# Key norms as quadrant products of one column, and the modifiers of keys and queries in one product

## The reference, cut to what matters

```python
def _modifier(x, w1, b1, w2, b2):
    h = jax.nn.gelu(x @ w1.T + b1, approximate=False)     # w1: 48 x 192, one for each of k, q, v   <-- touched
    return h @ w2.T + b2
xn = _ln(x, ln_in_g, ln_in_b)
k = xn @ Wk.T + 0.1 * _modifier(xn, km_w1, km_b1, km_w2, km_b2)      # 12 heads x 64; q and v alike
k = _ln(k.reshape(b, s, H, HD), lnk_g, lnk_b)
def step(M, kvq):
    k_t, v_t, q_t = kvq
    out_t = einsum('bhdk,bhk->bhd', M, q_t)
    kn = k_t / (norm(k_t, axis=-1) + 1e-06)               # one norm for each token and head        <-- touched
    pred = einsum('bhdk,bhk->bhd', M, kn)
    M_new = M - einsum('bhd,bhk->bhdk', pred + lr * (pred - v_t), kn)
    return M_new, out_t
```

## Time and profile before

| | |
|---|---|
| median of 3 runs | 1339.08 us (1338.1 to 1340.39) |
| profiled execution, its own time | 1343.92 us |
| its span | 1342.0 us |
| mean granted TensorE clock | 0.963 of full speed |
| busy over the span | PE 1232.0 us (92%), PEld 986.8 (74%), DVE 815.9 (61%), ACT 726.8 (54%), POOL 518.8 (39%) |
| chain that ended last, by engine | PE 34%, POOL 31%, issue 25%, DVE 5%, the rest 5% |
| products of `key_norms` | 384 instructions of 128x2, 45.8 us busy |
| products of `modifier` (L599) | 384 instructions of 128 columns, 28.0 + 27.9 us busy |

### The profile page before, as it was taken

One profiled execution on the slowest core, in us unless ns is written; L12 is line 12 of the kernel. 1 busy time (PEld: TensorE's weight loads), 2 busy tenths in 40 slices (PEclk: granted clock), 3 DMA queues, 4 the chain that ended last, 5 costly groups with the idle time before them and its releaser, 6 DMA issues.

```text
span 1342.0 us, 45313 instructions
## 1 busy us (share of the span) xinstructions
PE 1232.0 (92%) x17572; PEld 986.8 (74%) x17572; DVE 815.9 (61%) x2120; ACT 726.8 (54%) x1955; POOL 518.8 (39%) x689
## 2 busy tenths in 40 slices
PE   5898999999998588999999999999999999999975
PEld 5765666666665377888888888888888888888864
DVE  0136433333333266887877778787777878777752
ACT  0012222222222367777777777777777777777742
POOL 0000000000000355656565565556556555655521
PEclk8998999999998589999999999999999999999986
DMA  9888999999992012212221221122122112212210
GB/s 324 304 319 295 370 381 372 375 374 373 374 375 95 15 20 39 47 32 40 48 38 35 40 50 33 37 51 38 36 41 49 32 38 50 38 35 40 42 33 15
DMA packets 219995, 179.24 MB, mean 134 GB/s; under 512 B 164342, under 2 KB 189881, under 8 KB 219321
## 3 DMA queue, kind: packets, MB, share of 16 engines
q1 hardware_dynamic: 219818, 176.79, 41.3%
HBM read 154.72 MB, written 22.02 MB: 132 GB/s over the span
## 4 chain that ended last, share of the span: by engine, by line
PE 34%; POOL 31%; issue 25%; DVE 5%; SPq 2%; DMA 1%; ACT 1%; POOLq 0%; DVEq 0%; ACTq 0%
PE PS L438 29%; POOL region L1128 14%; POOL region L1111 5%; POOL region L1116 3%; POOL region L1122 1%; PE PS L514 1%; POOL region L1078 1%; POOL region L1094 1%; POOL region L1106 1%; SPq L308 1%; POOL region L1101 1%; PE PS L692 1%; PE PS L532 1%; PE PS L599 1%; POOL region L1091 1%
## 5 line engine op out<-in xcount | busy, mean ns | idle before, releaser
L438 PE MATMUL PS<-region 64*64 64x64 f32 (+6 forms) x5864 | 354.3, 287 | 20.7 <-DVE region L1176 13.6
L438 PEld LDWEIGHTS PS<-region 64*64 64x64 f32 (+3 forms) x5864 | 230.7, 139 | 119.6 <-issue 109.8
L1128 POOL TENSOR_TENSOR region<-region,powers 128x12 f32<-128x12 f32 x96 | 223.8, 2332 | 7.5
L1057 POOL TENSOR_TENSOR region<-region,powers 128x1 f32<-128x1 f32 x32 | 6.1, 192 | 408.5 <-DVE region L1236 408.5
L692 PEld LDWEIGHTS PS<-region 64*64 64x64 f32 x4608 | 145.1, 137 | 23.0 <-issue 18.9
L692 PE MATMUL PS<-region 64*64 64x64 f32 x4608 | 157.8, 223 | 1.4 <-ACT region L938 1.4
L438 PE MATMUL PS<-cw_hi,xr_hi 128*128 128x512 f32 (+3 forms) x384 | 149.3, 389 | 6.5 <-DVE region L1379 3.1
L905 ACT ACTIVATE region<-PS 128x512 f32<-128x512 f32 (+1 forms) x192 | 93.6, 488 | 84.3 <-PE PS L438 83.7
L438 PE MATMUL PS<-cw_lo,xr_hi 128*128 128x512 f32 (+3 forms) x384 | 130.8, 341 | 0.0
L438 PE MATMUL PS<-cw_hi,xr_lo 128*128 128x512 f32 (+3 forms) x384 | 130.5, 340 | 0.0
L832 ACT ACTIVATE region<-PS 128x384 f32<-128x384 f32 x32 | 15.7, 491 | 193.2 <-PE PS L438 193.2
(11 more groups left out here) (171 smaller groups left out, 2262.8 us busy)
## 6 DMA issues: line engine op xcount, KB each, us to landing
region<-in_Wq SPq DMA_DIRECT2D x32, 1152.0 KB, 5.8
region<-in_Wk SPq DMA_DIRECT2D x32, 1152.0 KB, 8.1
region<-in_Wv SPq DMA_DIRECT2D x32, 1152.0 KB, 7.7
region<-in_x SPq DMA_DIRECT2D x32, 384.0 KB, 6.7
n_scratch<-region SPq DMA_DIRECT2D x64, 192.0 KB, 3.4
region<-h_scratch SPq DMA_DIRECT2D x64, 96.0 KB, 2.0
region<-in_w SPq DMA_DIRECT2D x2, 2304.0 KB, 13.6
region<-i_scratch SPq DMA_DIRECT2D x256, 12.0 KB, 1.8
```

The lines of the kernel that those rows point to most:

```text
L438: return nc.tensor.matmul(dst, lhsT, rhs, start=first, stop=last)
L1128: pool.tensor_tensor(rs[:, cols], rs_var[:, cols], root[:, cols], ALU.pow).then_inc(S["rs_ready"], 1)
```

## The change

`key_norms` works on quadrants. For each of the 6 head pairs it makes 4 products: for each half of the tokens (64) and each of the two heads (64 partitions) the squared keys, 64x64, are the weights and one column of ones, 64x1, is the moving operand. Even heads go to bank 6 and odd heads to bank 7, columns 500 to 505 (`NORM_AT`). That is 24 products in place of 6. Since bank 7 is in turn used by `ffn_second(m)`, `key_norms` now waits for `f2_ready` (the copy of that result, `ffn_out(m)` on VectorE), and it has a `settled` ahead of it. `weigh_out`, which writes bank 7 too, now waits for `norm_copied` of the same step. `take_norm` is two copies of 6 columns, and what waited for one count of `norm_copied` waits for two.

`modifier` makes one product for keys and queries together: the weights have 112 columns (48 of the keys, 16 of zeros, 48 of the queries), and a second product of 48 columns is for the values. That is 4 products in place of 6. The GELU of the keys reads partitions 0 to 47 and writes partitions 64 to 111, as those of queries and values do. The host lays out weights and biases to suit.

One copy of 12 columns became two of 6. The diff, cut to its core:

```diff
@@ -49,6 +49,8 @@
 BLK_PITCH = BLK * SEQ + BLK
 HEAD_PITCH = NBLK * BLK_PITCH
 EPS = 1e-5
+NORM_AT = 500
+MOD_PAIR = R2 + MOD
 
 PIECE_BANK = (0, 1, 0, 7, 7, 7)
 PIECES = [(0, 512, 0), (512, 256, 0), (768, 256, 1), (1024, 512, 1), (1536, 512, 2), (2048, 256, 2)]
@@ -143,8 +145,8 @@
         p1w = sb("p1w", [P, CH, ATT])
         weff1 = sb("weff1", [HALF, ATT])
         weff2 = sb("weff2", [HALF + 1, ATT])
-        mod1a = sb("mod1a", [P, 3 * MOD])
-        mod1b = sb("mod1b", [R2, 3 * MOD])
+        mod1a = sb("mod1a", [P, MOD_PAIR + MOD])
+        mod1b = sb("mod1b", [R2, MOD_PAIR + MOD])
         gate_a = sb("gate_a", [P, ATT])
         gate_b = sb("gate_b", [R2 + 1, ATT])
         wo = sb("wo", [P, HEADS // 2, ATT])
@@ -584,7 +586,7 @@
 
             def turn_x(x, j):
                 pe.wait_ge(S["xh_ready"], x + 1)
-                need(pe, "norm_copied", upto(j))
+                need(pe, "norm_copied", upto(j, 2))
                 need(pe, "mod_ready", 3 * x)
                 for k, src in enumerate((xh, xn)):
                     nc.tensor.transpose(PS[:, 6, 2 * k * P:2 * k * P + P], src[:, 0:P], ident)
@@ -595,9 +597,9 @@
                 pe.wait_ge(S["xlin_copied"], 2 * x + 2)
                 pe.wait_ge(S["xgate_copied"], 2 * x + 2)
                 for part, (w, rows) in enumerate(((mod1a, P), (mod1b, R2))):
-                    for m in range(3):
-                        last = nc.tensor.matmul(PS[R2:R2 + MOD, 6, m * P:(m + 1) * P], w[:, m * MOD:(m + 1) * MOD],
-                                                x_aug[0:rows, part, :], start=part == 0 and m == 0, stop=part == 1,
+                    for i, (first, cols) in enumerate(((0, slice(0, MOD_PAIR)), (R2, slice(MOD_PAIR, MOD_PAIR + MOD)))):
+                        last = nc.tensor.matmul(PS[first:MOD_PAIR, 6, i * P:(i + 1) * P], w[:, cols],
+                                                x_aug[0:rows, part, :], start=part == 0 and i == 0, stop=part == 1,
                                                 skip_group_check=True)
                 last.then_inc(S["mod_mm"], 1)
 
@@ -652,8 +654,14 @@
             def key_norms(j):
                 pe.wait_ge(S["ksq_ready"], j + 1)
                 need(pe, "mod_ready", upto(j + 1, 3))
+                need(pe, "f2_ready", upto(j - 3))
+                settled(pe)
                 for i in range(HH):
-                    last = mm(PS[:, 6, 2 * i:2 * i + 2], ksq[:, i, :], head_ones)
+                    for e in range(2):
+                        tokens = slice(64 * e, 64 * e + 64)
+                        for odd, bank in enumerate((6, 7)):
+                            rows = slice(64 * odd, 64 * odd + 64)
+                            last = mm(PS[tokens, bank, NORM_AT + i:NORM_AT + i + 1], ksq[rows, i, tokens], head_ones[rows, odd:odd + 1])
                 last.then_inc(S["norm_mm"], 1)
 
             def grams(j, half):
@@ -746,6 +754,7 @@
                 pe.wait_ge(S["outT_ready"], 2 * l + 2)
                 need(pe, "raw_ready", upto(l + 2, 6))
                 need(pe, "f2_ready", l)
+                need(pe, "norm_copied", upto(l + 2, 2))
                 for i in range(HH):
                     last = mm(PS[:, 7, 0:ATT], outT[:, i, :], wo[:, i, :], i == 0, i == HH - 1)
                 last.then_inc(S["wo_mm"], 1)
@@ -922,9 +931,9 @@
             def gelu(x):
                 act.wait_ge(S["mod_mm"], x + 1)
                 rows = slice(R2, R2 + MOD)
-                for m in range(3):
-                    act.activation(x_aug[rows, 1 + m, :], PS[rows, 6, m * P:(m + 1) * P], ACT.Gelu,
-                                   bias=mod_bias[rows, m:m + 1]).then_inc(S["mod_ready"], 1)
+                for m, (at, i) in enumerate(((slice(0, MOD), 0), (rows, 0), (rows, 1))):
+                    act.activation(x_aug[rows, 1 + m, :], PS[at, 6, i * P:(i + 1) * P], ACT.Gelu,
+                                   bias=mod_bias[at, i:i + 1]).then_inc(S["mod_ready"], 1)
 
             def odd_heads(buf, i):
                 return buf.rearrange("p (g o d) -> p g o d", o=2, d=HD)[:, :, i, :]
@@ -1106,7 +1115,7 @@
                 pool.tensor_tensor(h2b[:, :], h2[:, :], beta[:, :], ALU.add).then_inc(S["h2b_ready"], 1)
 
             def key_lengths(j):
-                pool.wait_ge(S["norm_copied"], j + 1)
+                pool.wait_ge(S["norm_copied"], 2 * j + 2)
                 need(pool, "n2", j)
                 pool.tensor_tensor(norm[:, 1, :], norm[:, 0, :], square_root[:, 0:HEADS], ALU.pow).then_inc(S["n1"], 1)
 
@@ -1420,7 +1429,8 @@
             def take_norm(j):
                 dve.wait_ge(S["norm_mm"], j + 1)
                 need(dve, "n1", j)
-                dve.tensor_copy(norm[:, 0, :], PS[:, 6, 0:HEADS]).then_inc(S["norm_copied"], 1)
+                for odd, bank in enumerate((6, 7)):
+                    dve.tensor_copy(norm[:, 0, odd:HEADS:2], PS[:, bank, NORM_AT:NORM_AT + HH]).then_inc(S["norm_copied"], 1)
 
             def inverse_norms(j):
 
@@ -1558,8 +1568,11 @@
                           twice(a["attn_lnk_g"]), twice(a["attn_lnk_b"]), twice(a["attn_lnq_g"]), twice(a["attn_lnq_b"]),
                           a["ffn_b1"]], axis=1)
     d["vecs2"] = np.stack([a["attn_ln_in_g"][P:], a["attn_ln_in_b"][P:]], axis=1)
-    d["mod_bias"] = np.stack([a[f"attn_{m}m_b1"] for m in "kqv"], axis=1)
-    d["mod1T"] = np.concatenate([a[f"attn_{m}m_w1"].T for m in "kqv"], axis=1)
+    gap = np.zeros(R2 - MOD, np.float32)
+    pairs = [np.concatenate([a["attn_km_b1"], gap, a["attn_qm_b1"]]), np.concatenate([np.zeros(R2, np.float32), a["attn_vm_b1"]])]
+    d["mod_bias"] = np.stack(pairs, axis=1)
+    k1, q1, v1 = [a[f"attn_{m}m_w1"].T for m in "kqv"]
+    d["mod1T"] = np.concatenate([k1, np.zeros((ATT, R2 - MOD), np.float32), q1, v1], axis=1)
     d["modT"] = np.concatenate([np.concatenate([a[f"attn_{m}m_w2"].T, row(a[f"attn_{m}m_b2"])]) for m in "kqv"], axis=1)
     d["kqvT"] = np.concatenate([a["attn_Wk"].T, a["attn_Wq"].T, a["attn_Wv"].T], axis=1)
     d["gateT"] = np.concatenate([a["attn_Wg"].T, row(a["attn_bg"])])
```

4 lines of the change are left out of this document (2 added, 2 removed).

## The result

The changed kernel takes 1344.33 us (median of 14 runs, 1339.90 to 1348.92), the kernel before beside it 1340.65 (14 runs, 1338.10 to 1343.87): ratio 1.0029, 95% interval 1.0016 to 1.0041. It is 3.7 us slower, more than the 0.2% that I called no change. The profiled execution has a span of 1344.0 us, 2.0 above that of before; its own time is 1345.96.

What follows compares the result with a forecast made beforehand. The prediction took a closed loop of VectorE and GpSimd as the bound, with steps unchanged at 26.15 us. Start -1.55 and end +0.2 summed to -1.35 us, giving 1337.7 us, range 1334 to 1347.

Steps and rivals of the forecast that it cites:

- The steady step, and what bounds it: Middle of the second stage: a closed loop of VectorE and GpSimd sets the step, which stays at 26.15 us.
- The norms' products: Key norms on TensorE: the block takes 0.86 us, like `read_out`, in place of 1.35, saving 0.49 us.
- The first rival: Key norms: quadrants overlap only in pairs, block 1.5 us, time 1347; decides from a block of 1.14 us on; chance 0.10.
- The new wait in the middle: Middle steps: `key_norms` wait for `ffn_out` and start 0.84 us later, grams 0.35 us late; the step pays nothing.
- The cover: Middle steps: slack absorbing the late grams, 1.9 us at `take_a` and 0.28 us left at `take_e`.
- The modifiers: Middle steps on TensorE: a third of 12 instructions goes, gain 0.35 us of 1.64, at most 0.55, at worst nothing.
- The forecast's own price for a gain of nothing: Modifiers: if mode changes drain TensorE, they gain nothing and the sum is about 0.7 us more.
- The copies: VectorE: two copies of 0.17 us in place of one, covered by 1.5 us; nothing taken, upper side +3 in all.
- The start, "together -1.55 us": Start, chain through TensorE: modifiers of tile 0 save 0.7, of tile 1 0.35, norms 0.5; between -2.0 and 0.
- The third rival: TensorE idles more before the norms and its clock falls to 1.2 GHz in places: 1.5 us a step, +40; chance 0.04.
- The end, "+0.2": Steps without `moments_h`: norm copies at 1232.6 in place of 1232.12, partly covered by VectorE's next wait; between 0 and +0.5.

Runs made afterwards that it cites:

- before_moments: The kernel before with `moments_h` on VectorE moved from behind `ffn_out` to ahead of `invert_small` of the step before: 1339.54 us, ratio 1.0009.
- before_swap: The kernel before with `moments_h` ahead of `ffn_out` on VectorE in place of behind it: 1332.97 us, ratio 0.9940.
- before_wait: The kernel before with the new wait of `key_norms` for `ffn_out` alone, and the empty instruction with it: 1373.18 us, ratio 1.0250.

## Why the prediction was wrong, step by step

- **The steady step, and what bounds it:** right. 26.12 us against 26.15, and the undisturbed steps of `before_moments` (25.34) and of `before_swap` (25.87) show that the loop of VectorE and GpSimd set it.
- **The norms' products:** 0.69 us, forecast 0.86: even cheaper than `read_out`. 48 instructions in 0.69 us are 0.014 us for each. The Trainium skill, "TensorE: Matmul & The Clock Gate", section "Wait — 56ns, not 53.3ns?", puts the floor at about 25 ns; this trace stays below it once more. The first rival, with its 1.14 us, is refuted.
- **The new wait in the middle:** 0.78 us on average, forecast 0.84, and the grams 0.36 late, forecast 0.35. That the two agree so well is luck. The norms started 0.26 us after the end of `ffn_out` (1000.30, 1000.56) and not 0.08, and took 0.17 less than forecast. The cover held. That it would hold without the saving beside it, but for 0.2 us a step, I expected of `before_wait`, and it was wrong (some 1.2 us a step): the cover left out the clock.
- **The modifiers:** from their start to the end of the last, 1.57 us (1009.13 to 1010.70) in place of 1.64: a gain of 0.07, where I took 0.35 and at most 0.55. A third of the instructions went, and almost no time. The starts of the single instructions say where it went. Between two of one shape with 48 columns there are 0.11 us (979.50, 979.61), at a change of shape 0.20 (979.61 to 979.82; now 1009.33 to 1009.53, and at both other changes), and between the two with 112 columns 0.20 as well, their loads taking 0.17 us each in place of 0.12. Before there was one change of shape, now there are three. The trace of the kernel before had this price, and I did not look. The Trainium skill, "TensorEngine Tiling (Array Packing)", "Key Properties", says that a change of tiling mode drains TensorE, by which the gain could be nothing. The trace agrees that such a change costs time, 0.09 us over the usual distance, but no run shows that a drain is the reason. The forecast's own price for a gain of nothing, 0.7 us on the sum, was too small: it had taken 0.7 and 0.35 for the modifiers, 1.05.
- **The copies:** covered as forecast. The one instruction more brings a stall of 0.35 us into every eighth step, for which I had no term; over the whole stage it shows no net cost.
- **The start, "together -1.55 us":** 0.8 to 1.1 us were won up to the first `key_lengths`. At half clock the modifiers of tile 0 take 2.63 in place of 2.94, 0.31 and not 0.7; those of tile 1 0.06 and not 0.35. Then comes what the step had no word for. After the first `key_lengths` the chain leaves TensorE: it waits for the blocks of the inverse, and the time won turns into idle time before `form_e`. Behind it TensorE ran at half clock for 10.2 us, and step 4 is 3.0 to 3.4 us longer. **This is the step that failed.** It ended the sum where the gain was largest, and did not ask what TensorE meets when it is early. The third rival had the mechanism, but I looked for it in the steady step alone, and took as evidence against it a stretch near the end, not the start, where the chain's own rows were at half clock. Even that stretch was a sign for it: its 0.99 is full clock up to 1282.35 and half clock from there.
- **The end, "+0.2":** the numbers under it were right (copies 0.5 us late), but the cover was not there, and the delay comes in two of the steps without `moments_h`: 0.56 in step 31, 0.7 to 1.3 in step 33. This term was mis-sized: +0.2 taken, +1.3 to +1.8 measured.

The sum now: about -0.9 at the start, +3.0 in step 4, +1.3 at the end, and some of the single steps, for which the kernel before has one or two of its own. Counted directly, from the first `turn_x` to the last `key_lengths`, it is +4.6 in both pairs of profiles, against 3.7 (between 2.1 and 5.5) measured. The measured 1344.33 lies inside the range of 1334 to 1347 that I gave, but that range reached so far only for the first rival, which was refuted.
